# Cross attention of a decoder layer: masks of three of eight shifted score units, in all batches but the last, replaced by an integer product on GpSimd; one copy of the values a slot later

## The reference

```python
def xattn(mask, encodings, w_in, b_in, w_out, b_out, w_ct, b_ct, local_size=64):
    # mask = layernorm(x): 16 batches, E = 128 channels, T = 512 positions; H = 8 heads, d = 16
    q, k, v = split(transpose(mask) @ w_in.T + b_in)
    scores = einsum('bqhd,bkhd->bhqk', q, k) / sqrt(d)
    band = abs(idx[:, None] - idx[None, :]) <= local_size
    attn = softmax(where(band, scores, -inf))
    o = (einsum('bhqk,bkhd->bqhd', attn, v)) @ w_out.T + b_out
    y = relu(transpose(o)) * encodings
    return einsum('nit,io->not', y, w_ct) + b_ct
```

## Time and profile before

| | before |
|---|---|
| median of 3 runs | 1137.68 us (1136.1 to 1139.05) |
| the profiled execution | 1140.24 us |
| its span | 1138.4 us |
| PE busy | 1025.3 us, 90% |
| DVE busy | 791.7 us, 70% |
| ACT busy | 665.1 us, 58% |
| POOL busy | 602.7 us, 53% |

### The profile page before, as it was taken

One profiled execution on the slowest core, in us unless ns is written; L12 is line 12 of the kernel. 1 busy time (PEld: TensorE's weight loads), 2 busy tenths in 40 slices (PEclk: granted clock), 3 DMA queues, 4 the chain that ended last, 5 costly groups with the idle time before them and its releaser, 6 DMA issues. The chain is left out here.

```text
span 1138.4 us, 25188 instructions
## 1 busy us (share of the span) xinstructions
PE 1025.3 (90%) x9588; PEld 774.2 (68%) x9604; DVE 791.7 (70%) x1444; ACT 665.1 (58%) x1204; POOL 602.7 (53%) x586
## 2 busy tenths in 40 slices
PE   6689999999999999999977378999999998789996
PEld 5578778888888888888855156666666665344443
DVE  6577867666566665666753367787878765699995
ACT  5545555545545454554653236777777666578885
POOL 3564766657567565765663523353535345455552
PEclk9899999999999999999997689999999998899999
DMA  9133543432423423323552568878787751000001
GB/s 344 54 144 153 199 174 126 148 143 81 148 96 130 148 93 130 139 100 132 173 208 93 130 149 183 176 184 176 187 180 178 157 113 56 10 20 34 33 29 37
DMA packets 51144, 147.67 MB, mean 130 GB/s; under 512 B 10448, under 2 KB 24272, under 8 KB 39760
## 3 DMA queue, kind: packets, MB, share of 16 engines
q1 hardware_dynamic: 42288, 86.93, 28.7%
q0 software_dynamic: 8064, 58.72, 14.0%
q10 hardware_dynamic: 672, 0.40, 0.1%
HBM read 120.46 MB, written 25.17 MB: 128 GB/s over the span
## 5 line engine op out<-in xcount | busy, mean ns | idle before, releaser
L1583 DVE TENSOR_REDUCE mx<-Sm 128x4 f32<-128x768 f32 x128 | 122.5, 957 | 78.0 <-PE Sm L1078 75.8
L282 PE MATMUL Qb<-a_xTh,WqH 128*128 128x256 f32 x512 | 147.4, 288 | 1.1 <-DVE a_vl L800 0.8
L283 PE MATMUL Qb<-a_xTl,WqH 128*128 128x256 f32 x512 | 146.6, 286 | 0.0
L284 PE MATMUL Qb<-a_xTh,WqL 128*128 128x256 f32 x512 | 146.4, 286 | 0.0
L627 POOL TENSOR_TENSOR a_pr<-a_pr_plain,a_ph 128x512 fp32r<-128x512 f32 x64 | 83.4, 1304 | 111.1 <-ACT a_ph L447 110.9
L740 DVE TENSOR_TENSOR a_turned<-Qb,sinS 64x512 f32<-64x512 f32 (+1 forms) x144 | 94.9, 659 | 65.3 <-PE Qb L284 47.8
L1262 ACT ACTIVATE x_ex<-Se 128x768 f32<-128x768 f32 x128 | 103.7, 810 | 59.8 <-PE Se L1078 59.7
L459 ACT ACTIVATE Lb<-Lb 128x512 f32<-128x512 f32 x64 | 37.2, 582 | 173.5 <-PE Ob L354 173.5
L609 POOL TENSOR_TENSOR a_ql<-a_rot,a_qh 128x512 fp32r<-128x512 f32 x64 | 84.0, 1317 | 100.1 <-ACT a_qh L467 99.9
L367 PE MATMUL Yb<-a_WoH,a_oH 128*128 128x512 f32 x256 | 103.9, 406 | 4.2 <-POOL a_oN L605 4.2
L282 PEld LDWEIGHTS Qb<-a_xTh,WqH 128*128 128x128 f32 x512 | 99.8, 195 | 4.9 <-DVE a_vl L800 1.9
(11 more groups left out here) (204 smaller groups left out, 2784.6 us busy)
## 6 DMA issues: line engine op xcount, KB each, us to landing
a_WoH<-wo_parts POOLq DMA_DIRECT2D x28, 1024.0 KB, 5.1
a_WoL<-wo_parts POOLq DMA_DIRECT2D x28, 1024.0 KB, 7.1
x_K<-k_parts SPq DMA_DIRECT2D x32, 256.0 KB, 7.5
q_parts<-x_qp SPq DMA_DIRECT2D x16, 384.0 KB, 2.8
k_parts<-x_kp SPq DMA_DIRECT2D x16, 384.0 KB, 3.5
x_Q<-q_parts SPq DMA_DIRECT2D x16, 384.0 KB, 5.5
a_w_stage<-in_gateT SPq DMA_DIRECT2D x8, 704.0 KB, 4.7
x_w_stage<-in_gateT SPq DMA_DIRECT2D x8, 704.0 KB, 5.5
```

The costliest lines, as they stand in the source:

```text
L282: pe.matmul(out, w_hi(k), xTh[:, k, :], start=(k == 0), stop=False)
L283: pe.matmul(out, w_hi(k), xTl[:, k, :], start=False, stop=False)
L284: mm = pe.matmul(out, w_lo(k), xTh[:, k, :], start=False, stop=(k == KD - 1))
L1583: dve.tensor_reduce(mx[:, half, at:at + 4].rearrange("p (j a) -> p j a", j=2), Sm[:, :, 0:2 * WIN].rearrange("p j (a c) -> p j a c", a=2), ...
```

## The change

In `unit`, three of the eight `Se` units of a batch (`CUT` = 1, 2, 3), for all batches but the last, leave out the four mask matmuls, and their score matmuls write with `start=True` where they added before. What is then outside the band in `ex` is the exponential of an unmasked score. GpSimd multiplies the outer tiles of these units by a table of integers 0 and 1, `cap`, both sides read as int32, so that any bit pattern outside the band becomes zero (`outside_cut`). It is done in place, one instruction of 128 partitions by 4 x 2 x 64 elements for each unit. `values` waits for it (`ex_cut`). The table is made once by four DVE instructions at the start of the first step. In DVE's list the two halves of `head_values` move from slots 4 and 5 to slots 5 and 6.

```diff
@@ unit
-            def unit(S, rows, s, still, moving):
+            def unit(S, rows, s, still, moving, cut=False):
-                for j in range(2):
+                for j in range(0 if cut else 2):
...
-                                           start=False, stop=True, skip_group_check=True)
+                                           start=cut, stop=True, skip_group_check=True)
@@ shifted_scores
-                unit(Se, SHIFTED, s, K[b % 3], Q[b % 3]).then_inc(se_full, 1)
+                unit(Se, SHIFTED, s, K[b % 3], Q[b % 3], s in CUT and b < B - 1).then_inc(se_full, 1)
@@ values
                     wait(pe, v_ready, b + 1)
+                    wait(pe, ex_cut, len(CUT) * min(b + 1, B - 1))
@@ gpsimd
+            def outside_cut(b, s):
+                p, hf = divmod(s, 2)
+                wait(pool, ex_ready, SLOTS * b + s + 1)
+                sides = ex[:, (PAIRS * b + p) % RING, 4 * hf * WIN:4 * (hf + 1) * WIN].bitcast(I32).rearrange("p (j w c) -> p j w c", j=4, w=3)[:, :, 0:3:2, :]
+                pool.tensor_tensor(sides, sides, cap[:, :, :, :], ALU.mult).then_inc(ex_cut, 1)
...
                 if real(b + 2):
                     low(kp, kr, b + 2, k_mid, k_low)
+                if real(b):
+                    for s in CUT:
+                        outside_cut(b, s)
                 if b == -1:
+                    wait(pool, cap_ready, 4)
@@ vector
                 if b == -3:
+                    for j in range(4):
+                        dve.tensor_scalar(cap[:, j, :, :], t["band"][:, 4 * TS:6 * TS].rearrange("p (w c) -> p w c", w=2), -0.5 * BIG, None,
+                                          ALU.is_gt).then_inc(cap_ready, 1)
                     normalised(0)
...
+                    if s == 5 and real(b + 1):
                         head_values(b + 1, 0)
-                    if s == 5 and real(b + 1):
-                        head_values(b + 1, 1)
                     if s == 6 and real(b + 3):
                         rest(qp, qr, 0, b + 3, q_high, q_low, q_rest)
+                    if s == 6 and real(b + 1):
+                        head_values(b + 1, 1)
```

More of the change, by code:

```diff
@@ L9 @@
 BF16 = mybir.dt.bfloat16
+I32 = mybir.dt.int32
 ALU = mybir.AluOpType
@@ L307, in project_pair @@
                     if m < 2:
-                        pe.wait_ge(wq0_low, KD)
+                        pe.wait_ge(first_low, 2 * KD)
                     else:
@@ L682, in norm @@
                 ve, r1, r2, r3 = (t[name][:, lo:hi] for name in ("ve", "r1", "r2", "r3"))
-                at = 5 * i
+                at = 6 * i
                 if n == 0:
@@ L846, in step @@
                     if isinstance(g, int) and g == -1:
-                        dve.wait_ge(shift_done, 1)
+                        dve.wait_ge(norm_step, 6)
                     if isinstance(g, int) and g == 0:
-                        dve.wait_ge(shift_done, 2)
+                        dve.wait_ge(norm_step, 12)
                     for j in range(NG):
@@ L888 @@
 VALUE_TILES = ((0, 1, 2), (3, 4, 5), (6, 7))
+CUT = (1, 2, 3)
 def window(tile):
@@ L1010, in cross_and_ffn @@
         gate = sb("gate", [P, D], F32)
+        cap = sb("cap", [P, 4, 2, TS], I32)
         ctxb = sb("ctxb", [P, D], F32)
@@ L1472, in variance_root @@
             def variance_root(n, to, lo, hi):
-                wait(pool, n_var, n)
+                wait(pool, n_step, n)
                 pool.tensor_tensor(t[to][:, lo:hi], t["ve"][:, lo:hi], t["half"][:, 0:1].to_broadcast([P, hi - lo]), ALU.pow).then_inc(n_root, 1)
@@ L1490, in ffn_step @@
                 if b == 3:
-                    variance_root(3, "r1", FIRST, B)
+                    variance_root(6, "r1", FIRST, B)
                 if b == 5:
-                    variance_root(4, "r2", FIRST, B)
+                    variance_root(9, "r2", FIRST, B)
             for b in range(-3, B - 1):
@@ L1498, in _ @@
             variance_root(1, "r1", 0, FIRST)
-            variance_root(2, "r2", 0, FIRST)
+            variance_root(4, "r2", 0, FIRST)
             gated(B - 3)
@@ L1669, in variances @@
                 wait(dve, n_mv, hi)
-                dve.tensor_scalar(t["ve"][:, lo:hi], t["mv"][:, lo:hi, 1], EPS, None, ALU.add).then_inc(n_var, 1)
+                dve.tensor_scalar(t["ve"][:, lo:hi], t["mv"][:, lo:hi, 1], EPS, None, ALU.add).then_inc(n_step, 1)
             def variances_again(n, lo, hi):
+                at = n // 2 * 5
                 wait(dve, n_root, n)
-                dve.tensor_tensor(t["r2"][:, lo:hi], t["r1"][:, lo:hi], t["r1"][:, lo:hi], ALU.mult).then_inc(n_chain, 1)
-                wait(dve, n_chain, n)
-                dve.tensor_tensor(t["r3"][:, lo:hi], t["r2"][:, lo:hi], t["mv"][:, lo:hi, 1], ALU.mult).then_inc(n_chain, 1)
-                wait(dve, n_chain, n + 1)
-                dve.tensor_scalar(t["ve"][:, lo:hi], t["r3"][:, lo:hi], EPS, None, ALU.add).then_inc(n_var, 1)
+                dve.tensor_tensor(t["r2"][:, lo:hi], t["r1"][:, lo:hi], t["r1"][:, lo:hi], ALU.mult).then_inc(n_step, 1)
+                wait(dve, n_step, at + 2)
+                dve.tensor_tensor(t["r3"][:, lo:hi], t["r2"][:, lo:hi], t["mv"][:, lo:hi, 1], ALU.mult).then_inc(n_step, 1)
+                wait(dve, n_step, at + 3)
+                dve.tensor_scalar(t["ve"][:, lo:hi], t["r3"][:, lo:hi], EPS, None, ALU.add).then_inc(n_step, 1)
             def scales(n, lo, hi):
                 wait(dve, n_root, n)
-                dve.tensor_tensor(t["scale"][:, lo:hi], t["r1"][:, lo:hi], t["r2"][:, lo:hi], ALU.mult).then_inc(n_scaled, 1)
+                dve.tensor_tensor(t["scale"][:, lo:hi], t["r1"][:, lo:hi], t["r2"][:, lo:hi], ALU.mult).then_inc(n_step, 1)
             def rows_weighted(b):
@@ L1701, in rows_scale @@
                 wait(dve, f1_ready, b)
-                wait(dve, n_scaled, 1 if b < FIRST else 2)
+                wait(dve, n_step, 5 if b < FIRST else 10)
                 dve.tensor_scalar(bound[:, :], amax[:, :], scale, EPS, ALU.mult, ALU.max).then_inc(bound_ready, 1)
```

34 lines of the change are left out of this document (17 added, 17 removed).

## The result

The changed kernel takes 1145.26 us (median of 6 runs, 1142.63 to 1147.11), the kernel before 1139.89 in 6 runs (1136.1 to 1142.77). The ratio is 1.005, with a 95% interval of 1.0032 to 1.0068: **slower, by about 5.4 us**, where 2.0 us of gain were forecast. The profiled execution takes 1146.08 us against 1140.24, its span 1144.2 us.

What follows compares the result with a forecast made beforehand. TensorE was taken as the bound, with very little room behind it on DVE. Steps gain 0.6 + 1.0 + 8 x 0.13 = 2.6 us, the table costs 0.6: 1137.68 - 2.0 = 1135.7 us, 8-in-10 range 1131.0 to 1140.5.

Steps and rivals of the forecast that it cites:

- The moved copy on DVE: Behind slot 6's maxima, the copy's second half takes back 0.4 to 0.55 of 0.61 us; a step gains 0.13.
- Steps -1, 0 and 1: Steps 0 and 1 end with the keys' landing and gain nothing; the change was said to act in steps 0 to 14 alone.
- Step 2: This cross-attention step has no statistics, so DVE keeps up and it gains 0.6 us.
- The start: Four uncovered DVE table instructions ahead of the first normalised rows cost 0.15 us each, 0.6 us together.
- the 0.22 us of a cut unit: On TensorE, each unit without its four mask matmuls saves 0.22 us, 0.66 us a step.
- the normalised rows held by the gated output: In slot 4, DVE's rows wait for GpSimd and end at 776.7, covered by 0.3 us before the projection.
- step 13: Without the rest of the queries, 0.67 us is freed on DVE; this step and step 14 gain about 0.5 us each.
- steps 4 and 6: All but ended by the keys, which land 9.1 and 7.6 us after issue; they gain nothing.
- (1): TensorE keeps its gain, up to 0.6 us in 11 of steps 2 to 14: 1131.7 us; chance 0.25.
- (2): The keys end every step, leaving only the start's cost and the last steps' gain: 1137.3 us; chance 0.13.
- (3): Masks were free, the copy delays slot 7's maxima, +0.4 us in 11 steps: 1142.7 us; chance 0.08.
- (4): GpSimd's integer product is slow, from about 2.5 us, delaying normalised rows and projection: about 1150 us; chance 0.12.

Runs made afterwards that it cites:

- e10: The changed kernel with the table made behind the first normalised rows, nothing else; 1141.76 us, 1.003 of the kernel before.
- e1: The kernel before with only the copy of the values moved from slots 4 and 5 to slots 5 and 6; 1146.84 us, ratio 1.0058.
- e2: The changed kernel with the copy of the values back in slots 4 and 5; 1136.84 us, 0.9971 of the kernel before.
- e3: The changed kernel with DVE's statistics moved from slot 6 to slot 2 and the table behind the first normalised rows; 1135.22 us, 0.9966 of the kernel before.
- e4: The kernel before with the table and the 45 products added, all masks kept, copy in slots 4 and 5; 1143.1 us, ratio 1.0027.
- e5: e3 with the masks of batch 0 kept; 1137.09 us, 0.9985 of the kernel before.
- e6: The kernel before without the 45 mask groups and nothing in their place, so out-of-band scores stay in the sums; 1132.03 us, ratio 0.9945.
- e7: e5 with unit 0 cut as well, in batches 1 to 14; 1133.96 us, 0.9962 of the kernel before.
- e8: e5 with the copy of the values back in slots 4 and 5; 1138.07 us, 0.9981 of the kernel before.
- e9: The changed kernel with both halves of the copy in slot 5 and the table behind the first normalised rows; 1135.44 us, 0.9964 of the kernel before.
- e12: e3 with unit 0 cut too in batches 1 to 14; 1132.99 us, 0.9954 of the kernel before.
- e11: The kernel before with DVE's statistics moved from slot 6 to slot 2, nothing else; 1139.02 us, ratio 1.0.

## Why the prediction was wrong

**Which step failed.** It is the sum of the DVE tail, under "The moved copy on DVE". Relative to the start of step 5, forecast and measured:

| start of | forecast | measured |
|---|---|---|
| maxima of slot 6 | 14.60 | 14.55 |
| rest of the queries | 15.56 | 15.52 |
| second half of the copy | 16.23 | 16.30 |
| statistics | 17.09 | 17.19 |
| maxima of slot 7 | 17.69, at worst 17.82 | 17.92 |
| next `Sm` | 18.71, at worst 18.84 | 19.02 |

Up to the rest of the queries the chain is right within 0.05 us. Then the four gaps are each too small: rest to copy 0.78 for 0.67, copy to statistics 0.89 for 0.86, statistics to maxima 0.73 for 0.60, maxima to `Sm` 1.10 for 1.02. The 0.67 and 0.60 had been taken from a list in which the statistics followed the rest, and the 0.86 is the copy's row alone; a start-to-start time belongs to a pair of neighbours. The 1.02 is right inside a step: wherever DVE's maxima release an `Sm` there, its first row starts 0.97 to 1.02 us after theirs, in all 14 profiles. At the head of a step it is 1.10 or 1.11, in all 58 cases, and the one such case before stands at the head of step 0, with `Sm` at 671.37:

```profile
670.27 0.96 DVE L1583 TENSOR_REDUCE mx<-Sm 128x4 f32<-128x768 f32 x1 [0.15 <-PE Sm L1078]
```

All four together are 0.35 us. The forecast gain of a step was 0.13 us, so this turned it into a loss of 0.11. The mechanism and its place (first `Sm` released by the maxima, idle time ahead of it) were right; the size was not. Over steps 3 to 12 forecast and measurement are 3.1 us apart, out of 7.9 in all. Ten steps of 19.02 us would make 2.0 of them; 0.7 is a pause in slot 1 of step 4, and the rest some tenths in steps 8 to 10 and 12.

**Steps -1, 0 and 1** hold 3.35 us more that were put at nothing. Of these 0.76 is the moved copy in step -1, which the forecast skipped since no mask is removed there: the change's edits to DVE's list act in every step from -1 on. The rest is mostly the clock (about 1.3 us in step -1 and 1.2 in slot 3 of step 0) and a pause in slot 1 of step 1, with idle time of 0.77 us that no row explains and a slot of 3.35 us for 2.08. Part of it is chance: the same steps -1 to 1 take 54.26 us in the profile of before, 57.61 in that of after and 55.83 in e10, which differs from it by the table's place alone.

**Step 2** was to gain 0.6 us and gained 0.10. Its slot 2 took 3.22 us, where later steps take 2.71: one row of `values` matmuls lasts 1.29 us for 0.77. The same slot is stretched in e1, e2, e3, e4, e5, e6 and e10 and not in e7, e8, e9 and e12. The cause stays open.

**The start** cost 1.51 us for 0.6. The four table rows take 0.63, as forecast, and the normalised rows start 0.55 us after the first of them. The rest can't be laid to the change: the set-up ended 0.27 us later than before, and from the start of the normalised rows to the first `Sm` it is 20.66 us for 19.97, in the other profiles 20.25 to 20.85, also in e1 and e11, which have no table.

**Right:** the 0.22 us of a cut unit (0.23, 0.22 and 0.22 in slots 1 to 3); the whole 0.66 us once DVE's tail allows it (steps of 18.25 us in e6 and e9, where the forecast has 18.29 for TensorE alone); the product's 1.3 us; the normalised rows held by the gated output (1.01 us for a forecast 1.2), and that this is covered only because half of the copy left slot 4, which e2 and e4 show from the other side; step 13. For steps 4 and 6, said to be ended by the keys, the changed kernel shows the maxima instead; the keys came to it in the faster kernels.

**The rivals.** (1) TensorE does not keep its gain; e9 and e3 show what it would have taken. (2) The keys end no step of the changed kernel from 3 to 12. (3) The masks were not free, but this was the rival with the sign and nearly the mechanism: the same maxima of slot 7, too late by the copy. It was priced as if the saved 0.22 us decided; in truth the copy was under-priced, at 0.42 us a step where e1 shows 0.77. Its condition was off too: by its own figures the copy is made up for only from about 0.15 us saved per unit, not 0.07. e1, with all masks kept, is the nearest to that rival: 6.5 us. (4) The integer product is not slow: 1.92 us at most.

The Trainium skill (GPSIMD Engine Reference, "Engine selection") advised against elementwise products on GpSimd. The runs bear it out in part: table and products alone cost 2.8 us by e4, through the hold on DVE and not through GpSimd's own time, and are still worth it against the 6.6 us of e6. No run puts these products on VectorE, so the page's factor of two is not shown here.

## What to carry to other kernels

Price a move from the pairs of neighbours in the new order: a copy with a row of 0.86 us lengthened its chain by 1.13. When an engine runs near the limit in one slot, put work where the trace shows it idle (0.57 us ahead of the maxima here), not one slot later; the same change with both halves of the copy in slot 5 (and the table a little later) measured -0.36% for +0.5%. Test the parts of a change apart: this one was a gain of 0.29% and a loss of about 0.8%, and its sum hid both.

## What was new of the hardware

- An in-place integer product of 128 x 512 elements on GpSimd takes 1.27 to 1.92 us, median 1.33, about as long as the float one.
- DVE's normalised rows (0.52 us alone) are held until a GpSimd product that overlaps them ends, and take 0.82 to 1.13 us in steps 2 to 12; in e2, where the copy and the maxima follow without room, slot 5 is longer by 0.16 to 0.36 us.
- Start-to-start times on DVE depend on the rows around: maxima behind statistics 0.60 us where the statistics follow the rest of the queries (e9), 0.72 where they follow the copy (e1); statistics behind the rest 0.65, copy behind the rest 0.79.
- From the start of the maxima to the start of the `Sm` they release are 1.10 or 1.11 us at the head of a step and 0.97 to 1.02 inside one; their row is 0.96.
- Masks taken off an engine that waits anyway lengthen its wait (1.04 to 1.42 us), and in six of seven kernels its clock fell to the lower level right after.
- TensorE pauses in the middle of a row of matmuls, seldom, at other places in each profile, with nothing in the trace to explain it: idle time of 0.17 to 0.77 us, and a slot up to 1.27 us longer. This stays open.
